# Building an edge-count matrix on TensorE: strips of 25 rows against pairs of strips of 12 rows

## The chip, the cores and the metric

One core of one Trainium2 chip runs the kernel. The metric is device time in microseconds (us). The kernel before takes 369.93 us, the median of 3 runs (369.87 to 371.19).

## The reference, cut to what matters

```python
# x [1250, 512]; src, dst [40000], dst sorted and denser at low rows (1250 * u**2)
h   = relu(layernorm(x) @ W1 + b1) @ W2 + b2          # 512 -> 256 -> 512
x   = x + h + segment_sum(h[dst], src, 1250)          # row = src, col = dst
n   = layernorm(x)
gate = softmax(n @ W_gate + b_gate); thr = sigmoid(n @ W_thr + b_thr) * 0.25
w   = max(gate - thr, 0); w = w / sum(w)
x   = x + sum_e w[:, e] * (n @ W_exp[e] + b_exp[e])   # 8 experts, 512 x 512
```

The segment sum is computed as a product with a count matrix A: A[d, s] is the number of edges from d to s, plus one on the diagonal for h itself. The kernel builds A from the edge list.

## The kernel before, in words

**Prologue** (L657 to L724 on VectorE, L1004 to L1046 on TensorE). The 40,000 edges lie in 320 chunks of 125. From each chunk's smallest and largest `dst` VectorE marks which chunks touch which block of 25 rows of A (`above`, `below`, `hit`, `hit_idx`), TensorE turns the marks, and a dozen tiny operations make a table `wtab`: for each block the first chunk and the number of steps. The keys of all edges (`src % 250` and `5 * dst + src // 250`) are turned to lie with an edge per partition (`keys`).

**Counting** (`compare` on VectorE, `count` on TensorE, `block_out` on ScalarE, a loop on SyncE). A is made in 50 blocks of 25 rows by 1250 columns. In PSUM such a block is [125, 250]: partition 5 * row + s // 250, column s % 250. For each chunk of a block VectorE compares the keys with two running-number tables (L771): `places[..][0:128]` gives a one-hot of the partition and `places[..][128:384]` one of the column, 384 elements a chunk, `int16` in, `float16` out, up to 4 chunks in an instruction. TensorE multiplies the two one-hots (L1108: 128 columns of weights, 250 moving columns) into a PSUM bank. `STEPS` says how many instructions of how many chunks a step has; a register loop runs the steps of the table. Eight one-hot buffers (`hot`) let VectorE run ahead by two to four blocks. L1100 adds the diagonal. ScalarE copies the finished block to one of five buffers `counts` (L525) and writes the positions of the block five places ahead (`positions`, L493); SyncE moves it by one DMA (L368) into its 25 rows of a tile of A, `a_t` (3 buffers of [125, 1250]).

**In between** stand, on TensorE, ten slots of the hidden layer (`next_slot`: L1056, L1058, L1029) in the first seven blocks, and from block 10 on the product of a finished tile with the hidden rows (`aggregate`, L1070, float32, six matmuls a tile, spread over five blocks); on VectorE the norms' statistics (`first_norm`), four block sums (`block_sum`) and the column sums of A (`column_sum`, L796). An aggregate of tile i starts with block 5 * i + 10. The order on each engine is written out by hand; there is no scheduler.

**After the last block** its DMA lands, VectorE adds the last tile to the column sums, TensorE makes the degrees (L1133) and the last aggregates, and the second layer, norm, gate and experts follow (from 142 us to the end), which the change leaves as they are.

The loop on SyncE, which the prediction speaks of:

```python
for w in range(NW):                                  # 50 blocks
    i, q = w // WPT, w % WPT
    sp.wait_ge(win_out, w + 1)
    ...
    sp.dma_start(a_t[i % 3][q * WIN:(q + 1) * WIN, :].rearrange("p (h l) -> p h l", h=HI),
                 counts[q][0:WIN * HI, :]).then_inc(win_moved[q], 16)
```

Of the kernel before, what the change touches and what calls it, by code (L numbers as in the profile page):

```python
# [30 lines left out]
def gnn_moe(nc, x, src, dst, W1, b1, W2, b2, Wg, bg, Wt, bt, We, be, out):  # L31
# [12 lines left out]
    WIN = 25  # L44
    HI = 5
    LO = 250
    SW = HI * LO
    WPT = 5
    NW = TILES * WPT
    PART = 4  # L50
    STEPS = ((1, (4, 4, 4, 4)), (2, (3, 3, 3, 3)), (4, (4, 4, 4, 4)), (6, (4, 4, 4)), (9, (4, 3, 3)), (18, (4, 4)),
             (30, (3, 3)), (NW, (3, 2)))
    FIXED = ((1, 2), (2, 1), (NW, 0))
    EARLY = 9
    LAG = 5
    AHEAD = FIXED[0][1] * sum(STEPS[0][1])
    PADS = AHEAD + sum(STEPS[0][1]) - 1
    SEG = 128
    SEGS = 3
    REC = 2 * SEGS  # L60
    HOT = SEGS * SEG
# [4 lines left out]
    assert R * TILES == N and R == WPT * WIN and SW == N and CH * EP == NE  # L66
    assert WIN * HI <= SEG and LO <= 2 * SEG and LO % WIN == 0 and 2 * HI == TILES
    assert D == BANK and ROWS <= 128 and CH <= BANK and KC * SW <= 5 * BANK
    assert (CH + PADS + 1) * REC * WORD < 2 ** 24 and (CH + PADS + 1) * REC < WORD and KC * SW <= 5 * BANK

    with ExitStack() as ctx:
# [36 lines left out]
        self_pos = sb("self_pos", [128, SEG + HI - 1], F16)  # L108
        self_lo = sb("self_lo", [128, 2 * LO - WIN], F16)


        iota_pos = sb("iota_pos", [EP, PART, SEG], I16)
        iota_lo = sb("iota_lo", [EP, 2 * SEG], I16)
        win_base = sb("win_base", [EP, NW])
        places_all = sb("places", [128, WPT * PART * HOT], I16)
        places = [places_all[0:EP, q * PART * HOT:(q + 1) * PART * HOT].rearrange("p (c h) -> p c h", c=PART) for q in range(WPT)]
        base_row = sb("base_row", [ROWS, NW])
        last_row = sb("last_row", [ROWS, NW])
        step_col = sb("step_col", [NW, 1])
        step_inv = sb("step_inv", [NW, 1])  # L120
        first_end = sb("first_end", [NW, 1])
        step_half = sb("step_half", [NW, 1])
# [31 lines left out]
        below = sb("below", [ROWS, GJ, NW])  # L154
        above = sb("above", [ROWS, GJ, NW])
        hit = sb("hit", [ROWS, GJ, NW])
        hit_idx = sb("hit_idx", [ROWS, 2, GJ, NW])
        wmax = sb("wmax", [NW, 2])
        wtmp = sb("wtmp", [NW, 1])
        wfirst = sb("wfirst", [NW, 1])  # L160
        wcount = sb("wcount", [NW, 1])
        wsteps = sb("wsteps", [NW, 1])
        wcols = sb("wcols", [NW, 3])
        wfirsts = sb("wfirsts", [1, NW])
        wtab = sb("wtab", [1, 2 * NW], I32)
        keys = sb("keys", [EP, (CH + PADS) * REC], I16)
        HOTS = 8
        split = sb("split", [128, HOTS * PART * HOT], F16)
        hot = [split[0:EP, b * PART * HOT:(b + 1) * PART * HOT].rearrange("p (c h) -> p c h", c=PART) for b in range(HOTS)]

# [5 lines left out]
        xn = [sb(f"xn{i}", [R, D]) for i in range(2)]  # L176
# [5 lines left out]
        counts = [sb(f"counts{i}", [SEG, LO]) for i in range(WPT)]  # L182
        late = sb("late", [128, 4 * SW])
        a_t = [late[0:R, i * SW:(i + 1) * SW] for i in range(3)]
        a_sum = late[0:R, 3 * SW:4 * SW]
        assert KD * N <= 4 * SW
# [13 lines left out]

        s_hi = places_all[:, 0:PAIRS * 4 * 2 * 128].bitcast(F16).rearrange("p (j c k t) -> p j c k t", j=PAIRS, c=4, k=2)
# [11 lines left out]
        assert 2 * KD * N <= HOTS * PART * HOT  # L213
        xhi = split[:, 0:KD * N].rearrange("p (k n) -> p k n", k=KD)
        xlo = split[:, KD * N:2 * KD * N].rearrange("p (k n) -> p k n", k=KD)
        assert 2 * KD * N + 128 <= HOTS * PART * HOT
# [28 lines left out]
        lo_ready, self_base, self_ready = sem("lo_ready"), sem("self_base"), sem("self_ready")  # L245
# [3 lines left out]
        wcols_ready, wrows_ready, wtab_ready = sem("wcols_ready"), sem("wrows_ready"), sem("wtab_ready")  # L249
# [3 lines left out]
        first_ready = sem("first_ready")  # L253
        x_turned, x_t_ready = sem("x_turned"), sem("x_t_ready")
        r_done, r_ready = sem("r_done"), sem("r_ready")
        pos_ready = sem("pos_ready")
        hot_ready = [sem(f"hot_ready{p}") for p in range(4)]
        hot_used = [sem(f"hot_used{p}") for p in range(4)]
        step_base, step_ready, step_prep = sem("step_base"), sem("step_ready"), sem("step_prep")
        win_done, win_out = sem("win_done"), sem("win_out")  # L260
        win_moved = [sem(f"win_moved{q}") for q in range(WPT)]
# [24 lines left out]
        CONSTS = 7  # L286
# [12 lines left out]
        def parts_of(w):  # L299

            return next(parts for end, parts in STEPS if w < end)

        def fixed_of(w):

            return next(n for end, n in FIXED if w < end)

        def hot_at(w, p):

            if w < EARLY:
                return 4 * (w % 2) + p  # L310
            return 2 * ((w - EARLY + 2) % 4) + p

        def freed_by(w):

            return w - 2 if w < EARLY + 2 else w - 3 if w < EARLY + 4 else w - 4

        def moved(eng, tile):

            for q in range(WPT):
                eng.wait_ge(win_moved[q], 16 * (tile + 1))  # L320
# [17 lines left out]
        def _(sp):  # L338
# [973 lines left out]
```

## Time and profile before

| | |
|---|---|
| median of 3 runs | 369.93 us (369.87 to 371.19) |
| the profiled execution, its own time | 369.96 us |
| its span on the core | 368.2 us |
| busy share of the span: TensorE, VectorE, ScalarE, GpSimd | 95%, 85%, 35%, 15% |
| first compare / last `counts` copy / last strip landed | 13.7 / 131.6 / 137.9 us |

Times in the trace count from the start of the span. A busy share is an average over stages. TensorE's busy time counts overlapping matmuls as pipelined, so the distance between starts says more than a record's length. SPq, DVEq and PEq are the sequencers of SyncE, VectorE and TensorE: what they spend on registers, table loads and on issuing DMAs.

### The profile page before, as it was taken

What the parts mean: (1) busy time and instruction counts of PE and PEld (TensorE: products, weight loads), DVE (VectorE), ACT (ScalarE), POOL (GpSimd) and SP (SyncE); (2) the same over time, 40 slices, a digit from 0 to 9 for tenths busy, and PEclk for the clock granted to TensorE, in tenths of its full rate; (3) what the DMA queues carried; (4) which work ended last, traced back from release to release, by engine and by line L of the source; (5) the groups of instructions that cost most, each with busy time, mean ns of one, the idle gap of its engine ahead of it and who ended that gap; (6) DMA issues with size and microseconds to landing.
All of it is one profiled execution on the core that took longest, in us unless ns stands there. A gap on an engine that the chain in (4) does not pass through costs nothing.

```text
span 368.2 us, 7339 instructions
## 1 busy us (share of the span) xinstructions
PE 351.1 (95%) x2542; PEld 269.7 (73%) x2542; DVE 314.0 (85%) x565; ACT 127.9 (35%) x224; POOL 56.2 (15%) x83
## 2 busy tenths in 40 slices
PE   2999999999999989999999999999999999999995
PEld 1777787656656645457767888888888888888884
DVE  6799997999999878898686888889888888888764
ACT  5844354655679502377731313003030030210000
POOL 7000000000000000063632313050140500500000
PEclk9999999999999999999999999999999999999999
DMA  8971010222222250003000003030030300000133
GB/s 223 214 239 39 16 42 29 74 68 76 79 74 78 84 170 6 0 2 121 3 0 2 0 6 112 0 116 2 1 116 2 114 2 1 2 2 0 44 119 121
DMA packets 16273, 22.06 MB, mean 60 GB/s; under 512 B 2188, under 2 KB 9235, under 8 KB 16236
## 3 DMA queue, kind: packets, MB, share of 16 engines
q1 hardware_dynamic: 15820, 21.05, 19.4%
q10 hardware_dynamic: 416, 0.53, 0.6%
q8 instruction: 21, 0.34, 0.4%
q14 instruction: 16, 0.13, 0.1%
HBM read 12.77 MB, written 2.56 MB: 42 GB/s over the span
## 4 chain that ended last, share of the span: by engine, by line
PE 81%; DVE 10%; issue 3%; DMA 2%; DVEq 2%; ACT 1%; ACTq 0%
PE ps_g L1220 10%; PE ps_g L1221 10%; PE ps_g L1222 10%; PE ps_w L1108 9%; PE ps_g L1070 9%; DVE split L771 3%; PE ps_g L1056 3%; PE ps_a L1220 2%; PE ps_a L1222 2%; PE ps_a L1221 2%; PE ps_w L1221 2%; PE ps_w L1222 2%; PE ps_w L1220 2%; PE ps_g L1146 2%; DVE x_sb L854 2%
## 5 line engine op out<-in xcount | busy, mean ns | idle before, releaser
L771 DVE TENSOR_TENSOR split<-places,keys 125x1536 f16<-125x1536 int16 (+2 forms) x125 | 91.0, 794 | 4.3 <-PE ps_w L1108 1.9
L944 DVE SCALAR_TENSOR_TENSOR x_sb<-ps_g,weight_s,x_sb 125x256 f32<-125x256 f32 (+1 forms) x142 | 75.1, 546 | 19.6 <-PE ps_g L1222 18.4
L1220 PE MATMUL ps_g<-wb_hi,places 128*128 128x256 f16 x212 | 57.8, 273 | 0.1
L1221 PE MATMUL ps_g<-wb_lo,places 128*128 128x256 f16 x212 | 57.8, 273 | 0.0
L1222 PE MATMUL ps_g<-wb_hi,r_sb 128*128 128x256 f16 x212 | 57.8, 273 | 0.0
L1108 PE MATMUL ps_w<-split 125*128 125x250 f16 x402 | 53.7, 270 | 2.4 <-DVE split L771 1.8
L1108 PEld LDWEIGHTS ps_w<-split 125*128 125x128 f16 x402 | 36.7, 97 | 21.0 <-DVE split L771 8.4
L1070 PE MATMUL ps_g<-late,r_sb 125*128 125x512 f32 (+3 forms) x120 | 49.3, 516 | 1.7 <-DMA late<-counts 1.7
L574 ACT ACTIVATE wb_hi<-stage 128x512 f16<-128x512 f32 x7 | 4.4, 628 | 99.1 <-PE ps_g L1222 48.8
L1220 PE MATMUL ps_g<-wb_hi,split 128*128 128x256 f16 x142 | 38.7, 273 | 0.0
L1222 PE MATMUL ps_g<-wb_hi,split 128*128 128x256 f16 x142 | 38.7, 273 | 0.0
L1221 PE MATMUL ps_g<-wb_lo,split 128*128 128x256 f16 x142 | 38.7, 273 | 0.0
L493 ACT ACTIVATE places<-iota_pos,win_base 125x512 int16<-125x512 int16 x50 | 35.7, 714 | 0.0
L525 ACT ACTIVATE counts<-ps_w 128x250 f32<-128x250 f32 x50 | 19.0, 379 | 28.5 <-PE ps_g L1070 23.5
L1070 PEld LDWEIGHTS ps_g<-late,r_sb 125*128 125x128 f32 x120 | 19.5, 191 | 9.7 <-issue 9.0
L1220 PEld LDWEIGHTS ps_g<-wb_hi,places 128*128 128x128 f16 x212 | 20.8, 98 | 3.2 <-DVE x_sb L944 0.6
L442 POOL TENSOR_TENSOR t_sum<-stage 128x512 f32<-128x512 f32 x6 | 7.6, 1273 | 99.5 <-DVE wb_lo L837 87.1
L1221 PEld LDWEIGHTS ps_g<-wb_lo,places 128*128 128x128 f16 x212 | 20.7, 98 | 2.6
L1222 PEld LDWEIGHTS ps_g<-wb_hi,r_sb 128*128 128x128 f16 x212 | 20.7, 98 | 2.4
L944 DVE SCALAR_TENSOR_TENSOR x_sb<-ps_a,weight_s,x_sb 125x256 f32<-125x256 f32 x36 | 17.3, 481 | 4.3 <-PE ps_a L1222 3.7
L1056 PE MATMUL ps_g<-w_sb,x_t 128*125 128x256 f32 x80 | 19.6, 388 | 0.0
L465 POOL MEMSET split<- 128x4 f16 x1 | 0.1, 102 | 124.1 <-ACT counts L525 124.1
(223 smaller groups left out, 665.5 us busy)
## 6 DMA issues: line engine op xcount, KB each, us to landing
stage<-in_L_ffn_W_exp_dram SPq DMA_DIRECT2D x8, 1024.0 KB, 6.0
late<-counts SPq DMA_DIRECT2D x50, 122.1 KB
x_sb<-in_x_dram SPq DMA_DIRECT2D x5, 448.0 KB, 10.3
out_dram<-x_sb SPq DMA_DIRECT2D x10, 224.0 KB
w_sb<-in_L_gnn_W_dram SPq DMA_DIRECT2D x2, 512.0 KB, 10.0
out_dram<-x_sb ACTq DMA_DIRECT2D x10, 26.0 KB
b_sb<-in_L_gnn_b_dram SPq DMA_DIRECT2D x1, 250.0 KB
x_sb<-in_x_dram ACTq DMA_DIRECT2D x1, 208.0 KB
```

Of the source, the lines that this page charges most:

```text
L442: nc.gpsimd.tensor_tensor(t_sum[:, T1 - T1, :, :], b12, b11, ALU.subtract).then_inc(t_added, 1)
L493: nc.scalar.activation(places[w % WPT][:, :, 0:SEG], iota_pos[:, :, :], ACT.Identity, bias=win_base[:, w:w + 1], scale=1.0).then_inc(pos_r ...
L525: nc.scalar.activation(counts[q][:, :], ps_w[w % 2][:, 0:LO], ACT.Copy).then_inc(win_out, 1)
L771: nc.vector.tensor_tensor(hot[hot_at(w, p)][:, 0:n, :].rearrange("p c (k x j) -> p (c k) x j", k=SEGS, j=2), places[w % WPT][:, 0:n, :].re ...
L854: nc.vector.scalar_tensor_tensor(out=x_sb[:, i, :], in0=b2_sb[:, :], scalar=deg1[:, i:i + 1], in1=x_sb[:, i, :], op0=ALU.mult, op1=ALU.add ...
L944: nc.vector.scalar_tensor_tensor(out=x_sb[:, i, a:z], in0=bank[0:R, at:at + z - a], scalar=weight_s[:, expert_of(u), i:i + 1], in1=x_sb[:, ...
L1056: nc.tensor.matmul(r_bank[i % 2], x_t[i % XTS][:, k, :], w1_sb[:, k, :], start=(k == 0), stop=False)
L1070: g = nc.tensor.matmul(ps_g[:, a:z], r_sb[:, i, c * 128:(c + 1) * 128], a_t[i % 3][:, a - c * SW:z - c * SW], start=opens, stop=False, ski ...
L1108: mm = nc.tensor.matmul(bank[:, 0:LO], hot[hot_at(w, p)][:, c, 0:SEG], hot[hot_at(w, p)][:, c, SEG:SEG + LO], start=False, stop=False, ski ...
L1220: nc.tensor.matmul(out_cols, hi_x, wb_hi[par][:, q, k, :], start=(opens and k == 0), stop=False, skip_group_check=True)
L1221: nc.tensor.matmul(out_cols, hi_x, wb_lo[par][:, q, k, :], start=False, stop=False, skip_group_check=True)
L1222: mm = nc.tensor.matmul(out_cols, lo_x, wb_hi[par][:, q, k, :], start=False, stop=(k == 1), skip_group_check=True)
```

## The change

A is cut the other way. The source index is split in ten parts of 125 (`LO`, `HI`), so a strip of 12 rows by 1250 columns is a PSUM area of [120, 125], and two strips lie side by side in one bank: 54 groups, 50 of them with 24 rows, the first two and the last with one strip. A chunk needs 2 * 126 compared elements a strip, and its matmul has 125 moving columns. Both strips of a pair walk through the chunks with one loop: strip b starts a fixed number of chunks behind strip a (`behind`), and the table holds their common beginning.

A running number per partition is enough for both halves of the one-hot: `places_of` reads the same table twice, at 0 and at 10 * row. So the 50 `positions` writes and five `low_places` go, and ScalarE instead extends a table of 12,606 numbers in pieces of 700, five ahead of time and thirteen between blocks. A strip can straddle two tiles of 125 rows; it is then moved by two DMAs.

```diff
-    WIN = 25
-    HI = 5
-    LO = 250
+    WIN = 12
+    HI = 10
+    LO = 125
...
+    FIXED = ((1, 2, (6, 6)), (2, 1, (4, 4)))
+    LOOP = ((1, (5, 5), 0), (2, (4, 4), 0), (3, (6,), 11), (4, (5,), 9), (5, (4,), 7), (10, (6,), 5), (13, (5,), 4),
+            (30, (4,), 3), (NG - 1, (3,), 2), (NG, (2,), 0))
...
+        def windows_of(g):
+
+            return (2 * g,) if g in (0, 1, NG - 1) else (2 * g, 2 * g + 1)
...
-            for w in range(NW):
-                i, q = w // WPT, w % WPT
-                sp.wait_ge(win_out, w + 1)
-                if q == 0 and i >= 3:
-                    sp.wait_ge(g_done, i - 2)
-                    sp.wait_ge(a_summed, max(i - 3, 1))
-                sp.dma_start(a_t[i % 3][q * WIN:(q + 1) * WIN, :].rearrange("p (h l) -> p h l", h=HI),
-                             counts[q][0:WIN * HI, :]).then_inc(win_moved[q], 16)
+            for g in range(NG):
+                q = g % RINGS
+                sp.wait_ge(win_out, g + 1)
+                for s, a, z, tile, at in MOVES[g]:
+                    if tile > begun:
+                        begun = tile
+                        sp.wait_ge(g_done, tile - 2)
+                        sp.wait_ge(a_summed, max(tile - 3, 1))
+                    sp.dma_start(a_t[tile % 3][at:at + z - a, :].rearrange("p (h l) -> p h l", h=HI),
+                                 counts[q][SHIFT + a * HI:SHIFT + z * HI, s * LO:(s + 1) * LO]).then_inc(win_moved[q], 16)
...
+            def table(k):
+                a, z = k * PIECE, min((k + 1) * PIECE, TABLE)
+                nc.scalar.activation(places_all[:, a:z], places_all[:, 0:z - a], ACT.Identity, bias=piece_base[:, k:k + 1],
+                                     scale=1.0).then_inc(places_ready, 1)
...
+            def places_of(v, n):
+
+                base = places_all[0:EP, 0:SEG]
+                return bass.AP(base.tensor, base.offset, [list(base.ap[0]), [0, n], [row_of(v) * HI, SEGS], [2, SEG // 2], [1, 2]])
...
+                        nc.vector.tensor_tensor(hot[hot_at(stage, p)][:, 0:n, :].rearrange("p c (k x j) -> p c k x j", k=SEGS, j=2),
+                                                places_of(windows[s], n),
+                                                keys[:, ds(key_at, n * REC)].rearrange("p (c k j) -> p c k j", k=SEGS, j=2).unsqueeze(3)
+                                                .broadcast_to([EP, n, SEGS, SEG // 2, 2]),
+                                                ALU.is_equal).then_inc(hot_ready[p], 1)
...
+                            mm = nc.tensor.matmul(bank[:, s * LO:(s + 1) * LO], one_hots[:, c, HOT - 128:HOT], one_hots[:, c, 0:LO],
+                                                  start=False, stop=False, skip_group_check=True)
```

The prologue changes with it. The marks are made for 108 strips (elements 200 to 432 in each of five operations). The chain of tiny operations on columns that ended in three small matmuls is now one reduction, two small matmuls, and ten operations on one partition (216, 108 or 54 elements), all behind the matmuls. The constants of the table are written by 31 small memsets on VectorE, at its very start, and 30 on GpSimd.

SyncE's program, around the DMAs of the counts. Before, one a block:

```order
L358 DMA bg_sb<-in_L_ffn_b_thr_dram 125x1
L349 DMA stage<-in_L_ffn_W_exp_dram 128x4x512 x2
L368 DMA late<-counts 25x5x250 x50
L349 DMA stage<-in_L_ffn_W_exp_dram 128x4x512
L375 DMA early<-in_L_ffn_b_exp_dram 8x512 x3
L349 DMA stage<-in_L_ffn_W_exp_dram 128x4x512 x5
```

and now:

```order
L409 DMA bg_sb<-in_L_ffn_b_thr_dram 125x1
L400 DMA stage<-in_L_ffn_W_exp_dram 128x4x512 x2
L422 DMA late<-counts 12x10x125 x10
L422 DMA late<-counts 5x10x125
L422 DMA late<-counts 7x10x125
L422 DMA late<-counts 12x10x125 x9
L422 DMA late<-counts 10x10x125
L422 DMA late<-counts 2x10x125
```

The pattern goes on to the end of the strips: 114 DMAs in place of 50.

TensorE's program in a late block, with a piece of the aggregate. Before:

```order
L1070 MATMUL ps_g<-late,r_sb 128x226
L1100 MATMUL ps_w<-self_lo,self_pos 128x250
L1116 TENSOR_LOAD wtab
L1116 UNCONDITIONAL_BRANCH
L1108 MATMUL ps_w<-split 128x250 x5
L1111 ISA
L1116 COMPARE_AND_BRANCH
L1070 MATMUL ps_g<-late,r_sb 128x286
```

and now, where a group straddles two tiles (L1153 is there only then):

```order
L1117 MATMUL ps_g<-late,r_sb 128x452
L1149 MATMUL ps_w<-self_lo,self_pos 128x250
L1153 MATMUL ps_w<-self_lo,self_pos 128x250
L1179 TENSOR_LOAD wtab
L1179 UNCONDITIONAL_BRANCH
L1168 MATMUL ps_w<-split 128x125 x6
L1171 ISA
L1179 COMPARE_AND_BRANCH
L1117 MATMUL ps_g<-late,r_sb 128x512
```

Five matmuls of 250 columns for 25 rows have become six of 125 for 24 rows; the rest of a block is the same.

## Rows read from the trace of the kernel before

**Rows 1.** The page, busy time of each engine over the span.

```profile
PE 351.1 (95%) x2542; PEld 269.7 (73%) x2542; DVE 314.0 (85%) x565; ACT 127.9 (35%) x224; POOL 56.2 (15%) x83
```

**Rows 2.** Windows: length; busy us of PE, PEld, DVE, ACT, POOL; clock, DMA share, GB/s.

```profile
12.60:42.00 29.40, 27.81 (x177) 21.85 (x176) 27.59 (x48) 14.52 (x31) 0.00 (x0) 1.00 0.46 132
42.00:61.80 19.80, 19.53 (x124) 15.86 (x122) 18.46 (x26) 9.26 (x24) 0.00 (x0) 1.00 0.13 36
61.80:100.00 38.20, 37.97 (x238) 24.44 (x236) 37.61 (x48) 22.29 (x46) 0.00 (x0) 1.00 0.24 70
100.00:132.00 32.00, 30.90 (x170) 19.01 (x169) 29.99 (x45) 22.34 (x42) 0.00 (x1) 1.00 0.27 81
```

**Rows 3.** Chain that ended last, in order of time: start us, us, what.

```profile
0.74 2.48 DMA dst_i<-in_dst_dram
...
122.33 0.54 PE ps_w L1108 x5
122.86 1.62 PE ps_g L1070 x4
...
131.97 5.90 DMA late<-counts
```

**Rows 4.** Groups by form, VectorE, 12 to 140 us: busy, mean ns.

```profile
L771 DVE TENSOR_TENSOR split<-places,keys 125x1536 f16<-125x1536 int16 x47 | 41.8, 951 | 3.4 <-PE ps_w L1108 1.9 <-ACT places L488 1.1 <-issue 0.3
L771 DVE TENSOR_TENSOR split<-places,keys 125x1152 f16<-125x1152 int16 x58 | 41.0, 751 | 0.9 <-issue 0.7
L796 DVE TENSOR_TENSOR late<-late 125x1250 f32<-125x1250 f32 x9 | 13.1, 1456 | 3.5 <-DMA late<-counts 3.5
L771 DVE TENSOR_TENSOR split<-places,keys 125x768 f16<-125x768 int16 x20 | 11.0, 550 | 0.0
```

**Rows 5.** Lines L368 and L383, SyncE's issues: ns min/median/max, first and last start.

```profile
L368 SPq DMA_DIRECT2D late<-counts x50: 742/742/931, 32.9 to 132.0; - x50
...
L383 SPq DMA_DIRECT2D out_dram<-x_sb x10: 317/317/359, 347.3 to 364.9; - x10
```

**Rows 6.** Timeline of VectorE, prologue and first compares: start us, us, what.

```profile
4.61 0.36 DVE L665 TENSOR_TENSOR above<-last_row,cmin 80x200 f32<-80x200 f32 x1
...
10.34 0.20 DVE L698 SCALAR_TENSOR_TENSOR wcount<-wmax,wfirst,ones 50x1 f32<-50x1 f32 x1
10.58 0.21 DVE L702 SCALAR_TENSOR_TENSOR wsteps<-wcount,step_half,step_inv 50x1 f32<-50x1 f32 x1
...
12.40 0.19 DVE L713 SCALAR_TENSOR_TENSOR wtab<-ps_a,wfirsts 1x50 int32<-1x50 f32 x1
13.68 3.56 DVE L771 TENSOR_TENSOR split<-places,keys 125x1536 f16<-125x1536 int16 x4 [1.09 <-ACT places L488]
17.16 1.21 DVE L744 SCALAR_TENSOR_TENSOR w_sb<-ps_g,w_sb 128x1024 f32<-128x1024 f32 x1
```

**Rows 7.** Timeline of TensorE, the gate's matmuls of 18 and 9 columns.

```profile
157.62 0.35 PE L1165 MATMUL ps_g<-wg,split 128*125 128x18 f16 x4
157.82 0.38 PE L1168 MATMUL ps_g<-wg,split 128*125 128x9 f16 x4
```

**Rows 8.** Lines L1108 and L1165, their weight loads: ns min/median/max.

```profile
L1108 PEld LDWEIGHTS ps_w<-split x402: 95/98/101, 15.1 to 130.2; 125*128 125x128 f16 x134
...
L1165 PEld LDWEIGHTS ps_g<-wg,split x40: 136/138/139, 157.2 to 182.9; 128*125 128x125 f16 x40
```

**Rows 9.** Timeline of SyncE's queue at the start.

```profile
0.74 0.38 SPq L339 DMA_DIRECT2D dst_i<-in_dst_dram  x1
1.18 0.41 SPq L340 DMA_DIRECT2D src_i<-in_src_dram  x1
```

**Rows 10.** Timeline of TensorE, the matmul that closes block 6.

```profile
59.18 0.17 PE L1123 MATMUL ps_w<-zeros 1*128 1x2 f16 x1
```

**Rows 11.** Windows of one us, columns as in rows 2, counting and tail.

```profile
125.00:126.00 1.00, 1.00 (x6) 0.41 (x5) 1.00 (x3) 0.00 (x0) 0.00 (x0) 1.00 0.33 106
...
136.00:137.00 1.00, 0.42 (x2) 0.00 (x0) 0.00 (x0) 0.00 (x0) 0.00 (x0) 1.00 1.05 374
```

More of the change, by code:

```diff
@@ L185, in gnn_moe @@
         a_sum = late[0:R, 3 * SW:4 * SW]
+        below, above, hit = (late[0:ROWS, k * GJ * NV:(k + 1) * GJ * NV].rearrange("p (j v) -> p j v", j=GJ) for k in range(3))
+        hit_idx = late[0:ROWS, 3 * GJ * NV:5 * GJ * NV].rearrange("p (a j v) -> p a j v", a=2, j=GJ)
         assert KD * N <= 4 * SW
@@ new lines, in row_of, with fixed_of, loop_of, size_of @@
+        def row_of(v):
+            return WIN * (v // 2) if v < 4 else WIN * (v - 2)
+        def fixed_of(g):
+            return next(((n, tuple((0, m) for m in parts)) for end, n, parts in FIXED if g < end), (0, ()))
+        def loop_of(g):
+            parts = next(parts for end, parts, behind in LOOP if g < end)
+            return tuple((s, m) for s in range(len(windows_of(g))) for m in parts)
+        def size_of(parts):
+            return sum(m for s, m in parts if s == 0)
+        def stage_of(g):
+            return g + sum(n for end, n, parts in FIXED if end <= g)
@@ new lines, in hot_at, with group_rows @@
+        def hot_at(stage, p):
+            return 2 * (stage % 4) + p
+        def group_rows(fill, *rows):
+            a = 0
+            for end, parts, behind in LOOP:
+                n, ahead = sum(parts), fixed_of(a)[0] * size_of(fixed_of(a)[1])
+                value_of = {"add_a": (n - 1) / 2.0 - CH - ahead, "add_b": (n - 1) / 2.0 - CH - ahead - behind, "first_b": float(behind),
+                            "inv": 1.0 / n, "size": float(n * REC * WORD), "base": float((FRONT + CH + ahead) * REC * (WORD + 1))}
+                for row, name in rows:
+                    fill(row, value_of[name], a, end)
+                a = end
@@ new lines, in behind_of, with table_part @@
+        def behind_of(g):
+            return next(behind for end, parts, behind in LOOP if g < end)
+        def table_part(g):
+            return -(-(row_of(windows_of(g)[-1]) * HI + SEG) // PIECE)
+        MOVES, MOVED, MOVED_BY, LAST = [], [], {}, {}
+        total = [0] * RINGS
+        for g in range(NG):
+            moves = []
+            for s, v in enumerate(windows_of(g)):
+                row, end = row_of(v), min(row_of(v) + WIN, N)
+                while row < end:
+                    z = min(end, (row // R + 1) * R)
+                    moves.append((s, row - row_of(v), z - row_of(v), row // R, row % R))
+                    row = z
+            MOVES.append(moves)
+            total[g % RINGS] += 16 * len(moves)
+            MOVED.append(total[g % RINGS])
+            for s, a, z, tile, at in moves:
+                LAST[tile] = g
+                MOVED_BY[tile] = list(total)
@@ L317, in moved @@
         def moved(eng, tile):
-            for q in range(WPT):
-                eng.wait_ge(win_moved[q], 16 * (tile + 1))
+            for q in range(RINGS):
+                eng.wait_ge(win_moved[q], MOVED_BY[tile][q])
         PRODUCT, READ = {}, {}
@@ L414, in _ @@
[L414 to L424 removed]
+            nc.gpsimd.memset(keys[:, 0:FRONT * REC], -1).then_inc(pads_ready, 1)
@@ L1120, in _ @@
-            for w in range(NW):
-                count(w)
-                if w < WPT + LAG:
-                    nc.tensor.matmul(ps_w[w % 2][:, 0:2], zeros[0:1, 0:128], zeros[0:1, 0:2], start=False, stop=True,
+                stage = stage_of(g)
+                steps, parts = fixed_of(g)
+                for f in range(steps):
+                    one_step(stage, parts)
+                    stage = stage + 1
+                    next_slot()
+                with pe.Fori(0, pe.value_load(wtab[0:1, NG + g:NG + g + 1])):
+                    one_step(stage, loop_of(g))
@@ new lines, in _ @@
+            pe.wait_ge(self_ready, 4)
+            begins = [LAST[i] + LAG for i in range(TILES)]
+            pieces = {}
+            for i in range(TILES - 1):
+                for n in range(len(cuts)):
+                    pieces.setdefault(begins[i] + min(n, 4), []).append((i, n))
+            for g in range(NG):
+                count(g)
+                if g not in pieces:
+                    nc.tensor.matmul(ps_w[g % 2][:, 0:2], zeros[0:1, 0:128], zeros[0:1, 0:2], start=False, stop=True,
```

434 lines of the change are left out of this document (208 added, 226 removed).

## The prediction, made before the changed kernel ran

> **What bounds the kernel now.** I read the page's busy times first: TensorE 95%, VectorE 85%, ScalarE and GpSimd far behind [rows 1]. That is an average, so the windows come next. The change touches 0 to 138 us, and there they show two engines that are both nearly full in each stretch: 27.8 and 27.6 us of 29.4, then 38.0 and 37.6 of 38.2, and 30.9 and 30.0 of the last 32.0 [rows 2]. The granted clock is 1.00, the level of 2.4 GHz, throughout. The chain of waits tells which of the two is last: up to about 42 us compares and norms on VectorE, from then on TensorE, where a late block is 0.54 us of counting and a piece of the aggregate, and at the end the last DMA, 5.90 us [rows 3]. The groups by form give VectorE's share: 125 compares, and an idle time before them of only 4.3 us in all [rows 4]. So a gain needs both engines relieved, and this change relieves both. Then I looked at who comes next. SyncE issues one DMA a block, each holds its queue for 0.742 us, 37.1 us in 99.8 [rows 5]. Nothing waits for it today.
>
> **Part 1, the prologue: later by 3.6 us.** Each of the five mark operations grows from 200 to 432 elements. 200 elements of float32 take 0.36 us and 1024 take 1.21, so an element costs 1.03 ns and each operation 0.24 us more [rows 6]: 1.2 us, all ahead of the keys, on which TensorE's transposes and then the small matmuls wait. Behind these matmuls stood 0.43 us of work (12.16 to 12.59); now there are eight operations that depend on each other. A dependent pair starts 0.24 us apart [rows 6]; with 0.22, 0.11 and six times 0.06 us for the elements, and two side operations of 0.13, that makes 2.9 us, 2.4 more. The seven tiny operations that go from ahead of the matmuls free nothing, as TensorE was turning x until then. The 31 memsets stand where VectorE waits for `dst` (0.74 to 3.22 us): 0.08 us each fits, 0.12 would cost 1.3 us. I take 0 and keep 1.3 for the range. GpSimd's 30 memsets and ScalarE's first five pieces are needed at 12 us or later, where both idled. The first compare moves from 13.7 to 17.3.
>
> **Part 2, compares: VectorE 18.4 us less.** The inputs are fixed, so the strips' chunks can be counted: 125 compares and 402 matmuls before, as the rows have, and 119 and 476 now. Records of 951, 751 and 550 ns for 4, 3 and 2 chunks [rows 4] give 0.20 us for 384 elements, 0.52 ns each, and 0.15 of fixed time, of which the next one covers 0.08: four records in a row take 3.48 us, 0.87 each [rows 6]. Before: 47 * 0.87 + 58 * 0.67 + 20 * 0.47 = 89.2 us. Now a chunk is 252 elements, 0.131 us: 18 of six chunks at 0.86, 12 of five at 0.73, 42 of four at 0.60, 46 of three at 0.46 and one of two: 70.8 us. This takes the rate for granted though the pattern has one dimension more; see rival D.
>
> **Part 3, counting on TensorE: 14.5 us less.** Five matmuls of 250 columns take 0.54 us [rows 3], 0.107 each, so 402 are 43.0 us. No row has 125 columns with new weights each time. From above the bound is 0.107. From below: 18 columns with loads of 138 ns start 0.05 us apart [rows 7, 8], and half of 250 columns is 0.052. Here loads are the shorter kind, 98 ns [rows 8]. I take 0.057, by the streaming time plus a little: 27.1 us, 15.9 less. Four more groups and nine straddling ones add 13 diagonals of 0.107. The Trainium skill (TensorE: Matmul & The Clock Gate, Back-to-back issue gap) gives about 81 ns for load and matmul pairs of 128 columns; by it counting would be 38.6 us, and only 3 us would be gained here. The gate's rows are against it, though they are eight in a row at most.
>
> **Part 4, ScalarE: nothing.** 50 position writes and five tables go, 18 pieces come. It was busy 35% [rows 1]; no wait of VectorE on positions stands in the chain after the start.
>
> **Part 5, SyncE: 50 DMAs become 114.** This is the step that I think decides. A pair of strips is two DMAs, and a strip that straddles two tiles three for its group. Price: the row of the same transfer, 0.742 us [rows 5], plus 0.04 between issues, as 1.18 stands to 0.74 + 0.38 [rows 9]: 0.785. The pattern (rows of the tile from ten partitions each) is the same kind, 12 rows from 120 partitions for 25 from 125. The nearest rows on either side are 0.317 (an output, both sides plain) and 0.931 (the first of the counts) [rows 5]. I take 0.742, since it was the median and the minimum of 50 of the same sort. From group 6 on that is 104 DMAs, 81.6 us. When is group 6 out? Block 6 closed at 59.2 [rows 10], with VectorE setting the pace. Its compares for these rows fall from 30.2 (27 of four chunks, 10 of three) to 19.4 us, and the start is 3.6 later: 52.0. So SyncE ends its issues at 133.6, the last one starts at 132.8. VectorE and TensorE would have been done at 117: 131.6 + 3.6 - 18.4 for the one, and much the same for the other. They wait: TensorE for PSUM banks, ScalarE for one of five buffers, these for SyncE.
>
> The Trainium skill (DMA: Bandwidth & Descriptors, Issuing engines are not separate DMA queues) calls the time to initiate a DMA "usually small relative to the DMA itself". By that it would not bind, which is rival B. The row says 0.742 us each, and a tile of 125 rows needs 11.4 of them, 8.9 us, where TensorE needs about 6.7 (31 * 0.057 + 0.6 + 4.2 of aggregates).
>
> **Part 6, the tail: 3.3 us less from a faster landing.** Today the last DMA takes 5.90 us, and in the stretch before it the engines' share is 0.33 while it can be 1.05 [rows 11]. A third is 5 of 16 engines, full all the time. The Trainium skill (DMA: Bandwidth & Descriptors, Why a DMA increments its semaphore by 16 and not by 1) says that a DMA runs on the largest number up to 16 that divides both outer sizes: 5 for 25 and 125, agreeing with the share, and 12 for 12 and 120. Bounds: 5.90 us, and 2.48 for a plain load on an idle queue [rows 3]. I take 2.5, for the last one has 20 packets and nothing queued: landed at 135.3 in place of 137.9.
>
> **The sum.** The landing of the last strip releases the last column sum, the degrees and all that follows, and nothing behind it changes. 135.3 - 137.9 = -2.6 us on the profiled execution's own 369.96 (which is within 0.03 of the median): **367.4 us**.
>
> **The rivals.**
>
> A, the forecast, chance 0.44: SyncE's issues set the pace at about today's price. 362 to 372 us, by 0.70 to 0.78 us an issue.
>
> B, chance 0.26: the issue is cheaper, as more engines with fewer packets each are served. Below 0.62 us a DMA SyncE keeps up, and the engines' savings come through: 3.6 - 18.4 with the landing's 2.6 gives **353 us**. For it: the price differs by the kind of transfer, 0.317 to 0.742 [rows 5]. Against: nothing shows what of the transfer makes it 0.742.
>
> C, the other side, chance 0.18: the issue is dearer, as it grows with the number of engines served (12 for 5). From 0.81 us a DMA (issue and gap) the landing is at 137.9 or later and the gain is gone; at the bound of 0.931 the 104 DMAs take 101 us, 19.4 more, **387 us**.
>
> D, chance 0.05: the compare's pattern of four dimensions falls to half the rate. 476 * 252 elements at 0.52 ns more are 62 us, on VectorE all visible: 353 + 62 = **415 us**. Against: pairs of 16-bit neighbours are kept on all three sides, as before.
>
> E, chance 0.07: counting does not get cheaper on TensorE, and a matmul of 125 columns takes 0.107 like one of 250. The change then doesn't do what it says: 476 * 0.107 is 50.9 us, 7.9 more than before, and with the prologue the end moves by about 9 less 2.6: **376 us**. By the 81 ns of the Trainium skill (TensorE: Matmul & The Clock Gate) it would be 11.5 us above B's TensorE, 364, or hidden in A.
>
> **How the numbers follow.** Half a per cent, 1.85 us, is about what a measurement of this kernel can tell from no change. A lies around 367.4 on both sides of that bound: 0.26 below 368.1, 0.12 within, 0.06 above. With B all faster, a hundredth each of C and E below the line, and the rest of C, D and E slower: faster 0.54, same 0.12, slower 0.34. The range reaches from B, 353 with a microsecond to spare, to 380: half of C (0.09), D and a little of E lie above, some 0.03 below. A's own range is 362 to 372.
>
> **What would show it.** Right: SyncE's row for the counts shows 114 issues of about 0.74 us one behind the other from about 52 us on; TensorE and VectorE show gaps of 20% or more in 60 to 130 us, ending with ScalarE's copies that wait for landed strips; compares of 1512 elements take 0.94 us, of 756 0.54; the first compare starts at 17.3; counting matmuls start 0.057 us apart; the last DMA takes 2.5 us. Wrong: issues well under 0.6 us and the last copy near 117 (B), or above 0.8 (C); records of 1.6 us for 1512 elements (D); starts of 0.1 us between counting matmuls (E). If the first compare is later than 18.6 us, the prologue was priced too low.

## The result, and the profile after

The changed kernel takes 383.04 us (median of 4 runs, 382.25 to 383.48) where the kernel before takes 370.06 us beside it: a ratio of 1.0342, with a 95% interval of 1.0314 to 1.0369. It is slower by 13.0 us. The prediction was 367.4 us, with a range of 352 to 380, and faster as the likeliest sign. Number and sign are wrong. The profiled execution took 383.21 us, with a span of 381.4 us.

The page has less work and more time. Busy times of the changed kernel, against [rows 1]:

```profile
PE 348.6 (91%) x2629; PEld 266.3 (70%) x2629; DVE 299.9 (79%) x588; ACT 106.6 (28%) x193; POOL 54.7 (14%) x102
...
PEclk9999999999998995799999999999999999999999
```

VectorE lost 14.1 us of work and TensorE 2.5, although part of TensorE's was done at half the clock: the second row is its granted clock in 40 slices (9 is 90% or more of 2.4 GHz), and the slices from 143 to 162 us have 5 and 7 where the kernel before has 9 throughout. The windows say where the engines stood still; the columns are those of [rows 2]:

```profile
12.60:42.00 29.40, 25.83 (x185) 21.91 (x185) 23.11 (x51) 9.83 (x26) 0.00 (x0) 1.00 0.48 136
42.00:61.80 19.80, 17.43 (x153) 14.13 (x151) 16.35 (x23) 7.41 (x19) 0.00 (x0) 1.00 0.13 32
61.80:100.00 38.20, 34.10 (x267) 20.77 (x264) 32.50 (x52) 16.70 (x35) 0.00 (x0) 1.00 0.27 66
100.00:132.00 32.00, 27.47 (x169) 15.60 (x170) 22.47 (x40) 11.71 (x23) 0.00 (x0) 0.95 0.28 70
...
144.00:146.00 2.00, 0.20 (x1) 0.23 (x2) 0.26 (x1) 0.00 (x0) 0.00 (x0) 0.60 0.44 50
146.00:158.00 12.00, 12.00 (x32) 7.84 (x32) 6.84 (x12) 0.00 (x0) 0.00 (x0) 0.50 0.23 85
```

From 61.8 to 132 us TensorE idles 8.6 us of 70.2, where it idled 1.3 before, and VectorE 15.2. Neither is full any more. SyncE is, though the busy times don't count it. (The 0.95 is a first, short drop of the clock: 0.57 from 120 to 124 us, behind 2 us with 0.57 us of work. SyncE's issues go on back to back through it.) Its own line, against [rows 5], and who waited for those transfers:

```profile
L422 SPq DMA_DIRECT2D late<-counts x114: 652/772/1393, 30.4 to 143.5; - x114
...
  DVE late L843: 18.1, 7
  ACT counts L558: 7.7, 8
  PEld ps_g L1117: 4.7, 1
  PE ps_g L1117: 4.0, 1
```

The chain of work that ended last shows the same at the end of the counting (start us, us, what). Behind the copy six issues hang on one another before the last DMA starts; it lands, and the tail of the first layer runs:

```profile
138.34 0.39 ACT counts L558
138.73 0.66 SPq L422
139.39 0.04 issue
139.44 0.77 SPq L422
...
143.51 1.94 DMA late<-counts
145.45 0.35 issue
145.80 3.75 PE ps_g L1117 x4
149.56 4.00 PE ps_a L1203 x20
153.55 4.89 PE ps_g L1117 x8
...
158.47 0.39 ACT early L628
```

So two things are lost. The last strip lands at 145.5 us instead of 137.9 (+7.6). And from there to the first copy of the finished product (`early`) it is 13.0 us, where it was 6.9 (137.9 to 144.8): +6.1, because all of it runs at a granted clock of 0.50, the level of 1.2 GHz. The four aggregates that take 3.75 us took 1.96 before. Together they make 13.7 us; the span grew by 13.2.

### The profile page after: what moved, and what is told of

The parts are those of the page before. It is cut to its first block, busy times and chain, and to the rows that moved or that the text cites. A ratio compares the mean times of both kernels' runs of the same rounds, so it can differ in the third digit from the quotient of the medians.

```text
span 381.4 us, 7568 instructions
## 1 busy us (share of the span) xinstructions
PE 348.6 (91%) x2629; PEld 266.3 (70%) x2629; DVE 299.9 (79%) x588; ACT 106.6 (28%) x193; POOL 54.7 (14%) x102
## 4 chain that ended last, share of the span: by engine, by line
PE 86%; issue 4%; DVE 4%; DMA 2%; SPq 1%; ACT 1%; DVEq 1%; ACTq 0%
PE ps_g L1117 13%; PE ps_g L1290 10%; PE ps_g L1291 10%; PE ps_g L1292 10%; PE ps_w L1168 7%; PE ps_g L1103 4%; PE ps_g L1216 3%; PE ps_a L1290 2%; PE ps_a L1291 2%; PE ps_a L1292 2%; PE ps_w L1291 2%; PE ps_w L1290 2%; PE ps_w L1292 2%; PE ps_w L1149 2%; PE ps_g L1256 1%
## 5 line engine op out<-in xcount | busy, mean ns | idle before, releaser
L809 DVE TENSOR_TENSOR split<-places,keys 125x756 f16<-125x756 int16 (+4 forms) x119 | 73.3, 680 | 11.1 <-PE ps_w L1168 7.8
L1117 PE MATMUL ps_g<-late,r_sb 125*128 125x512 f32 (+3 forms) x120 | 57.0, 582 | 13.2 <-issue 9.1
L1168 PEld LDWEIGHTS ps_w<-split 125*128 125x128 f16 x476 | 30.2, 99 | 19.7 <-DVE split L809 10.6
L1168 PE MATMUL ps_w<-split 125*128 125x125 f16 x476 | 37.4, 220 | 6.5 <-DVE split L809 5.8
L1117 PEld LDWEIGHTS ps_g<-late,r_sb 125*128 125x128 f32 x120 | 21.3, 208 | 22.4 <-issue 21.9
L558 ACT ACTIVATE counts<-ps_w 128x250 f32<-128x250 f32 (+1 forms) x54 | 20.1, 374 | 53.2 <-PE ps_g L1117 40.2
L843 DVE TENSOR_TENSOR late<-late 125x1250 f32<-125x1250 f32 x9 | 13.1, 1461 | 19.7 <-DMA late<-counts 18.1
L992 DVE SCALAR_TENSOR_TENSOR x_sb<-ps_a,weight_s,x_sb 125x256 f32<-125x256 f32 x36 | 17.3, 482 | 4.3 <-PE ps_a L1292 3.7
L1103 PE MATMUL ps_g<-w_sb,x_t 128*125 128x256 f32 x80 | 19.7, 390 | 0.0
```

The source lines that it names most:

```text
L558: nc.scalar.activation(counts[q][:, 0:cols], ps_w[g % 2][:, 0:cols], ACT.Copy).then_inc(win_out, 1)
L809: nc.vector.tensor_tensor(hot[hot_at(stage, p)][:, 0:n, :].rearrange("p c (k x j) -> p c k x j", k=SEGS, j=2), places_of(windows[s], n), k ...
L843: nc.vector.tensor_tensor(a_sum, a_t[0] if i == 1 else a_sum, a_t[i % 3], ALU.add).then_inc(a_summed, 1)
L992: nc.vector.scalar_tensor_tensor(out=x_sb[:, i, a:z], in0=bank[0:R, at:at + z - a], scalar=weight_s[:, expert_of(u), i:i + 1], in1=x_sb[:, ...
L1103: nc.tensor.matmul(r_bank[i % 2], x_t[i % XTS][:, k, :], w1_sb[:, k, :], start=(k == 0), stop=False)
L1117: g = nc.tensor.matmul(ps_g[:, a:z], r_sb[:, i, c * 128:(c + 1) * 128], a_t[i % 3][:, a - c * SW:z - c * SW], start=opens, stop=False, ski ...
```

## The experiments

Each ratio is against runs of the kernel before on the same chip, whose median was 369.4 to 370.1 us in every case; 383.0 us is the changed kernel of the result. Landings and copies are from the profiled execution of each.

**Who issues.** Three kernels leave the 114 DMAs as they are and hand the second strip of a pair to another queue. The core of the edit is a function `move(eng, g, strips)` that holds SyncE's loop body:

```diff
+            for g in range(NG):
+                sp.wait_ge(win_out, g + 1)
+                move(sp, g, (0,))
```

The first adds, behind ScalarE's copy of a group g that has two strips:

```diff
+                act.wait_ge(win_out, g + 1)
+                move(act, g, (1,))
```

> The changed kernel, but the second strip of each pair is moved by a DMA that ScalarE issues behind its own copy; SyncE keeps the first strips. Nothing else differs: the same 114 DMAs, the same bytes. Theory (SyncE's serial issues set the end of counting from 61.4 us on, 0.81 us for each DMA, and the gaps they leave on TensorE lower its clock in the tail): SyncE has about 61 issues left instead of 114, its row is no longer back to back, the last DMA lands at 131 to 136 us instead of 145.5, the granted clock stays near 1.00 behind it, and the time is 360 to 367 us. Rival one (the moving itself is what is slow: more packets over fewer engines): who issues doesn't matter, 380 to 384 us. Rival two (the compares and TensorE wait for each other through the one semaphore per stage, and SyncE only follows): also 380 to 384 us.

Measured: 378.74 us, 1.0254 [1.0225, 1.0282]. A miss: 4.3 us gained where 16 to 23 were expected. The waits between 60 and 160 us show why (engine, operand and line waited for: us in total, times, longest):

```profile
ACT counts L564 <- PE ps_g L1126: 29.1, 24, 2.6
DVE split L818 <- PE ps_w L1177: 15.4, 24, 2.9
PEld ps_w L1158 <- ACT counts L564: 15.3, 21, 2.4
...
PE ps_w L1158 <- ACT counts L564: 7.1, 8, 2.0
```

TensorE now waits for ScalarE's copies, its weight loads 15.3 us and its matmuls 7.1 us (the two waits overlap, so they don't add up): on ScalarE copy, 0.38 us, and issue, 0.78 us, stand one behind the other, and the counting has only two PSUM banks. The last copy was made at 143.0 us, no earlier than SyncE alone had got to the end. What was gained is the clock (0.991 on average instead of 0.976): landing to `early` was short again, 7.0 us.

The second makes the copy of group g first and then issues the strip of the group before:

```diff
-                act.wait_ge(win_out, g + 1)
-                move(act, g, (1,))
+                act.wait_ge(win_out, g)
+                move(act, g - 1, (1,))
```

> As in the run with ScalarE issuing the second strips (378.7 us), but it first makes the copy of the next pair and only then issues the DMA of the last one, so that a copy never waits for its own strips' issue. Theory (that run was held back by the chain copy, issue, copy on ScalarE): TensorE's waits for copies fall by half or more, and the time is 363 to 372 us. Rival (ScalarE's 0.4 + 0.8 us for each pair hold TensorE's two banks however they are ordered): 376 to 380 us.

Measured: 369.64 us, 0.9994 [0.996, 1.0027]. The same DMAs, the same two queues, only the order of copy and issue turned, and 9.1 us less. The weight loads' wait for copies fell from 15.3 us to 10.1, the matmuls' own from 7.1 to 3.1. The last issue was at 135.1 us.

In the third it is `pool.wait_ge(win_out, g + 1)` and `move(pool, g, (1,))`, with semaphores of its own for GpSimd's transfers.

> The changed kernel, but GpSimd, which is idle in this stage, issues the DMA of each pair's second strip, with semaphores of its own; ScalarE only copies, SyncE issues 61 of the 114. Same DMAs, same bytes. Theory, mended after the run in which ScalarE issued them (there TensorE's waits moved from SyncE to ScalarE's chain of copy, 0.38 us, and issue, 0.78 us, one behind the other): with neither SyncE nor ScalarE in the way TensorE is the bound; it has 69.6 us of work left at 61.8, so the last strip lands at 132 to 136 us and the time is 361 to 367 us, if GpSimd's issue takes under 1.3 us. Rival (the moving is what is slow, whoever issues): 377 to 384 us. Rival (an issue of GpSimd costs 1.5 us or more): its row is back to back, and the time is above 375 us.

Measured: 366.30 us, 0.9906 [0.9873, 0.994]. GpSimd's issues cost less than SyncE's and neither row is back to back:

```profile
L386 SPq DMA_DIRECT2D late<-counts x59: 673/772/1060, 30.5 to 129.6; - x59
L386 POOL DMA_DIRECT2D late<-counts x55: 570/572/735, 43.9 to 128.8; - x55
```

The last issue was at 129.6 instead of 143.5 us, and TensorE was busy 37.3 of the 38.2 us from 61.8 to 100. With the same transfers and bytes, the rival that the moving itself is slow has fallen; 16.7 us hung on who issues.

**Fewer issues.** Two kernels drop DMAs of second strips and keep all computing, so that rows of the matrix are stale:

```diff
+            if g % 2 == 0 and g >= 18:
+                moves = [m for m in moves if m[0] == 0]
             MOVES.append(moves)
```

This leaves out 19; with `if g >= 18` alone it is 38.

> The changed kernel without the DMA of the second strip in every other pair from the 18th on: 19 of the 114 DMAs are left out, so that those rows of the count matrix are stale. Compares, matmuls and copies are all still made. Theory: each DMA left out takes its issue of 0.81 us off SyncE's chain, 15.4 us in all, as long as TensorE isn't the bound first; the last DMA lands at 130 to 136 us, and with the clock kept the time is 361 to 369 us. Rival (the handshake of VectorE and TensorE sets the pace): 380 to 384 us.

> The changed kernel without the second strip's DMAs from the 18th pair on: 38 of 114 are left out (19 in the run before of this kind, which took 365.6 us). Theory: SyncE is no longer near the bound, 38 issues of 0.81 us would be 31 us, but only some 11 to 14 us can be had, since TensorE is full then: 357 to 366 us, and little under the run with 19 left out. Rival (SyncE is the only bound down to there): 350 us or less.

Measured: 365.61 us, 0.9875 [0.9838, 0.9911], with 19 left out, and 365.96 us, 0.9884 [0.9828, 0.9939], with 38. The first 19 are worth 17.4 us, the next 19 nothing. In the profiled execution with 19 left out the last DMA lands at 134.1 instead of 145.5 us (11.4 of their 15.4 us of issue; the last copy, at 131.5, is now what it waits for), and landing to `early` takes 8.9 instead of 13.0 us. That is the floor at which TensorE binds (busy 36.3 of the 38.2 us from 61.8 to 100), and GpSimd's version stands on it.

**The same bound in the kernel before.** There each block's DMA is cut by rows:

```diff
-                sp.dma_start(a_t[i % 3][q * WIN:(q + 1) * WIN, :].rearrange("p (h l) -> p h l", h=HI),
-                             counts[q][0:WIN * HI, :]).then_inc(win_moved[q], 16)
+                for a, z in ((0, 8), (8, 16), (16, WIN)):
+                    sp.dma_start(a_t[i % 3][q * WIN + a:q * WIN + z, :].rearrange("p (h l) -> p h l", h=HI),
+                                 counts[q][a * HI:z * HI, :]).then_inc(win_moved[q], 16)
```

> The kernel before with each block's one DMA cut into three by rows (8, 8 and 9 rows of the matrix): 150 DMAs instead of 50, the same bytes, everything else the same. Theory (an issue costs SyncE about 0.74 us plus 0.04 whatever it moves, one after the other): 43 blocks are left at 59 us, 129 issues at 0.78 to 0.81 make 101 to 105 us, so the last DMA lands near 162 us instead of 138, and the time is 390 to 402 us. Rival (an issue's price goes with the partitions or bytes that it describes): at a third of 0.74 us the row is as before, and the time is 369 to 373 us.

Measured: 399.68 us, 1.0814 [1.0781, 1.0847].

```profile
L369 SPq DMA_DIRECT2D late<-counts x150: 668/693/832, 32.8 to 160.9; - x150
...
  ACT counts L526: 35.0, 27
  DVE late L797: 29.4, 7
```

A third of the partitions costs 0.693 us instead of 0.742. Between these two the price is one for each DMA and hardly goes with what it moves. 132 issues start between 59.8 and 160.9 us, 0.77 apart, and ScalarE and VectorE, who waited for almost nothing here before, now wait for landed strips.

> The kernel before with the DMAs of every second block issued by GpSimd. SyncE has 25 issues there instead of 50 and waited for nobody. Theory (more issuers help only where SyncE's issues are the bound): no change, 368 to 371 us. Rival (GpSimd's queue lands DMAs faster, or relieves something else, whatever the kernel): 362 to 366 us, which would take the gain of the run with GpSimd in the changed kernel away from the theory.

Measured: 373.80 us (370.51 to 375.76), 1.0122 [1.0082, 1.0161]. GpSimd as a second issuer brings no gain where SyncE wasn't the bound, so the gain in the changed kernel isn't some virtue of that queue. That it costs 1.2% was not expected. The four times go with their mean granted clocks (0.999 at 370.5 us, 0.984 at 375.8); why it falls more often here is open. The groups show the compares as long as before, 951 ns for 1536 elements.

**The start of SyncE's stretch.** In the changed kernel the hidden layer's matmuls are cut to a quarter of their depth:

```diff
-                for k in range(KD):
+                for k in range(1):
                     nc.tensor.matmul(r_bank[i % 2], x_t[i % XTS][:, k, :], w1_sb[:, k, :], start=(k == 0), stop=False)
```

> The changed kernel with the hidden layer's matmuls cut to the first of their four parts of the depth, so that its values are wrong and each of the ten slots between the early groups costs TensorE about 1.2 us less (8 float32 records of 1.99 us become 2 of 0.5). Theory: in the changed kernel TensorE's slots, one behind each early group and 3.3 us long, set when the group of 60.2 us is out, and SyncE's back-to-back stretch starts there; so that copy comes 6 to 9 us earlier, the last DMA lands as much earlier (137 to 140 instead of 145.5), and the time is 374 to 378 us. Rival (VectorE's compares or the keys set the first stage, as the prediction took it): the copy stays within 2 us of 60, and the time at 381 to 384 us. Rival (SyncE doesn't set the second stage): the copy moves, the landing doesn't.

Measured: 379.07 us, 1.0267 [1.0228, 1.0305]; against the changed kernel 4 us less, short of the 5 to 9 expected. The copy of group 7 came at 54.19 instead of 60.18 us, as expected, but the last issue at 140.5, only 3.0 earlier. Groups 8 and 9, which have no slot ahead of them, still came 2.3 and 2.6 us apart, because VectorE's compares and block sums now set the pace (TensorE, and its wait for the compares in brackets):

```profile
54.03 0.28 PE L1149 MATMUL ps_w<-self_lo,self_pos 128*128 128x250 f16 x1
54.95 0.50 PE L1168 MATMUL ps_w<-split 125*128 125x125 f16 x6 [0.64 <-DVE split L809]
55.80 0.50 PE L1168 MATMUL ps_w<-split 125*128 125x125 f16 x6 [0.35 <-DVE split L809]
```

SyncE could follow these; back to back it went from 59.6 us on, with 97 issues left instead of 101. That is 1.0 us of start and 3.3 of issues; 1.3 went again because the issues took a little more each (0.843 us apart instead of 0.829). So in the changed kernel TensorE's slots set when group 7 is out, and VectorE stands close behind them.

**The clock.** 33 matmuls on constants, read by nobody, fill two of TensorE's waits in the changed kernel, 10 ahead of tile 8's first aggregate and 23 ahead of tile 9's:

```diff
+                        for m in range(10):
+                            nc.tensor.matmul(ps_w[(g + 1) % 2][:, 0:384], self_pos[:, 0:128], self_lo[:, 0:384], start=True, stop=True)
...
+            for n in range(23):
+                nc.tensor.matmul(ps_w[0][:, 0:384], self_pos[:, 0:128], self_lo[:, 0:384], start=True, stop=True)
             aggregate(TILES - 1, 0, 2)
```

> The changed kernel with 33 matmuls of 384 columns on constants added, whose results nobody reads: 10 ahead of tile 8's first aggregate and 23 ahead of tile 9's, where TensorE stood waiting for DMAs. The DMAs are left as they are. Theory: the last DMA lands at 145 to 147 us as in the changed kernel, but the granted clock stays at 1.00 behind it, the first four aggregates of tile 9 take 2.0 us instead of 3.75, and the time falls by 5 to 6 us, to 377 or 378. Rival (the lower clock has another cause than the idle time, or costs nothing on the path): 382 to 384 us, clock at 0.50 as before.

Measured: 379.06 us, 1.0254 [1.0227, 1.0281]: 4.0 us less by work that is thrown away. The timeline of TensorE there:

```profile
142.35 3.90 PE L1206 MATMUL ps_w<-self_lo,self_pos 128*128 128x384 f16 x23
146.09 1.88 PE L1117 MATMUL ps_g<-late,r_sb 125*128 125x512 f32 x4
147.81 2.24 PE L1210 MATMUL ps_a<-ones,late 125*125 125x1 f32 x20
149.91 4.42 PE L1117 MATMUL ps_g<-late,r_sb 125*128 125x226 f32 x8
```

The last issue is at 143.4 as before; the four aggregates take 1.88 us, not 3.75, the degrees 2.24, not 4.20. `early` starts at 154.4 instead of 158.5. The time is 1 us above what was expected, for the clock did not stay up: the last eight ran mostly at the lower level, which is the part of 6.1 us that did not come back. And that fall has no gap ahead of it:

```profile
138.00:150.00 12.00, 12.00 (x63) 7.50 (x64) 9.33 (x12) 0.66 (x2) 0.26 (x4) 1.00 0.44 130
150.00:152.00 2.00, 2.00 (x7) 1.29 (x7) 1.88 (x4) 0.00 (x0) 0.00 (x0) 0.69 0.00 0
```

So the wait for the last strip explains 4.0 of the 6.1 us; the cause of the rest is open.

**What is left.** The version with GpSimd still fell to 0.50 between 138 and 144 us. Eight more such matmuls go into it, four ahead of tile 9's first aggregate and four behind its last.

> The run in which GpSimd issues the second strips (366.3 us), with 8 matmuls of 384 columns on constants whose results nobody reads: 4 ahead of tile 9's first aggregate, where TensorE waited 0.5 us, and 4 behind its last one, where it waits for the copies. There the clock had fallen to 0.50 from 138 to 144 us. Theory (the lower clock comes of too little work in TensorE's stretch before it): it stays at 1.00, the last aggregates and the second layer's first four matmuls are 3 us shorter together, less up to 1 us for what the eight matmuls delay: 363 to 365 us. Rival (another 0.7 us of work doesn't change the level): 366 to 367.5 us.

Measured: 364.95 us, 0.9878 [0.9847, 0.9909], clock 1.00 in the profiled execution, `early` at 139.2 instead of 140.4 us. In time it can't be told from the version without the eight (0.9906 [0.9873, 0.994]). The same kernel once more, beside the next one:

> The same kernel as the one with GpSimd's issues and 8 added matmuls (364.95 us, 0.9878 of the kernel before), once more, on the chip of the run beside it: 364 to 367 us, 0.984 to 0.992.

Measured: 365.79 us, 0.9907 [0.9869, 0.9945]. In this profiled execution the clock fell to 0.50 from 138 to 140 us in spite of the eight, and `early` came at 140.6: that they keep the clock up is not shown. Its windows before 62 us are those of the changed kernel: TensorE idles 5.8 us there, 5.7 of them in matmuls that wait for compares (the 12.3 us expected for the next run adds to these the weight loads' waits, which overlap them). The suspects are the groups with two steps, so their first step goes ahead of the loop:

```diff
-    FIXED = ((1, 2, (6, 6)), (2, 1, (4, 4)))
+    FIXED = ((1, 2, (6, 6)), (2, 1, (4, 4)), (3, 1, (6,)), (4, 1, (5,)), (5, 1, (4,)))
```

with `fixed_of` giving the parts of both strips, and slots and norms at fixed steps in groups 0 and 1 only.

> The version with GpSimd's issues and the 8 added matmuls (364.95 us), and in groups 2 to 4 the first of the two steps is taken out of the loop and gets a stage of buffers of its own, so that VectorE can write the second step while TensorE still has the first or the hidden layer's slot before it. Nothing is computed anew. Theory (in these three groups the two engines wait for each other, some 1.1 to 1.5 us of TensorE's idle time in each, 12.3 us on compares before 62 us in all): TensorE's waits for compares before 62 us fall by 3 to 4 us and the time to 361 to 363 us. Rival (VectorE is then late with the next groups, and the wait only moves): 364 to 366 us.

Measured: **360.54 us** (359.56 to 362.63), 0.9751 [0.9713, 0.9789], and 5.2 us under its neighbour. The waits before 62 us, first the neighbour's, then its own:

```profile
PEld ps_w L1179 <- DVE split L820: 7.2, 8, 1.8
DVE split L820 <- PE ps_w L1179: 7.2, 4, 2.7
...
PE ps_w L1179 <- DVE split L820: 5.7, 8, 1.4
```

```profile
PEld ps_w L1180 <- DVE split L820: 2.5, 3, 1.7
...
PE ps_w L1180 <- DVE split L820: 1.7, 2, 1.3
```

The copy of group 7, behind the last slot, comes at 55.3 instead of 60.2 us, and TensorE is busy 19.7 of 19.8 us from 42 to 61.8. This version beats both kernels, by 9.4 and about 22 us.

## Why the prediction was wrong

Its mechanism was the right one, rival A's and C's alike: SyncE's issues, one behind the other, set the end of the counting. It is shown from three sides (another issuer, fewer issues, the same bound made in the kernel before). Three steps of the sum failed: the start of SyncE's stretch in part 5 (with "VectorE setting the pace"), the price of an issue there, and "nothing behind it changes" in the sum. The first two alone turn the sign (378.0, with the landing 377.4 us); the third takes the time out of the range.

- **Part 5, the start, +6.2 us.** The text has group 6 out at 52.0 because VectorE's compares fall from 30.2 to 19.4 us, "with VectorE setting the pace". It didn't after the change, and the prediction's own reading of the chain had TensorE last from about 42 us on, so already in the kernel before block 6 stood on TensorE. The windows of the first stage had both engines nearly full [rows 2], and TensorE's ten slots of the hidden layer there, 2.3 to 2.7 us each, are not what the change removes. Group 6 was copied at 56.9 and group 7 at 60.2, where SyncE's stretch began, with 101 issues to go; the prediction's count has it there at 54.4. The run with shorter slots moved group 7 by 6.0 us, to 54.2, close to the 54.4 that the prediction had with VectorE's pace. And part of it is new: in groups 2 to 4 the steps of a loop share one stage of buffers, so each engine waits for the other. The last version got 4.9 us of that stage back by unrolling them.
- **Part 5, the price, +4.4 us.** 0.785 was assumed, 0.742 and a gap of 0.04. (The row that the gap was read from has 0.06: 1.18 less 0.74 and 0.38 [rows 9]. With it the price would have been 0.80.) The issue is 0.772 in the median, 0.03 above the row of before, and 0.04 lies between two, 0.812; with some issues of up to 1.39 us the 100 intervals from 60.58 to 143.51 average 0.829. The last issue starts at 143.5, not 132.8, and 10.7 is what these two terms make. Rival C put the point of no gain at 0.81 a DMA and its cause with the number of engines served; the cut blocks speak for a price nearly fixed for each DMA.
- **Part 6, the landing, -0.6 us.** 1.94 us against 2.5 predicted and 5.90 before. The gain is there, but the last DMA moves 2 rows of the matrix where it moved 25, so that more engines share a transfer is not what it shows.
- **The tail, +6.1 us, a term that the sum doesn't have.** "Nothing behind it changes" holds for the instructions, not for the clock. The prediction itself forecast gaps of 20% on TensorE and read a granted clock of 1.00 in every window [rows 2], but never asked what the gaps would do to it. TensorE had 0.20 us of work in 144 to 146 us and none in 142 to 144, and the clock then stood at 0.50 for 12 us. The run with fillers gave 4.0 us back; the rest went with a second fall, of which the cause is open. The Trainium skill (TensorE: Matmul & The Clock Gate, Part 1: The HAM clock gate) describes a gate that goes by how busy the engine has been recently. This trace agrees at the wait from 142 to 145.8 us; the fall of the run with fillers, behind 12 full us, is not explained by it.
- 367.4 + 6.2 + 4.4 - 0.6 + 6.1 is 383.5; the profiled execution took 383.2.
- **Part 1** was 0.7 us too high: the first compare came at 16.58 us, not 17.3. The 31 memsets cost nothing.
- **Part 2** held. The compares keep VectorE busy for 73.3 us against 91.0 before, 17.7 less where 18.4 were predicted, and rival D is out:

```profile
L809 DVE TENSOR_TENSOR split<-places,keys 125x1008 f16<-125x1008 int16 x42 | 25.6, 679 | 2.8 <-PE ps_w L1168 2.4 <-issue 0.2
L809 DVE TENSOR_TENSOR split<-places,keys 125x756 f16<-125x756 int16 x46 | 22.4, 549 | 1.7 <-issue 1.0 <-PE ps_w L1168 0.6
L809 DVE TENSOR_TENSOR split<-places,keys 125x1512 f16<-125x1512 int16 x18 | 16.2, 942 | 3.8 <-PE ps_w L1168 2.0 <-issue 1.7
```

- **Part 3** held: six counting matmuls of 125 columns take 0.33 us in the chain, 0.055 each against 0.057 predicted. Rival E is out. The 81 ns for a pair of load and matmul (the Trainium skill, TensorE: Matmul & The Clock Gate, Back-to-back issue gap) don't hold for these rows of six to twelve pairs; the measurement decides.
- **Part 4** held, ScalarE is at 28%.
- The rule set against part 5 (the Trainium skill, DMA: Bandwidth & Descriptors, Issuing engines are not separate DMA queues), that initiating is usually small beside the transfer, doesn't describe this case: 0.77 us of issue for transfers that land in 1.94 us (the last) or 2.61 (the one issued at 61.4 us).
- **Rival B's** 353 us was not to be had by cheaper issues. With issues out of the way the kernel takes 366 (three kernels, 365.6 to 366.3), and the last copy comes at 129.3 us (with GpSimd), not near 117. B's sum let all that VectorE saves come off the end. TensorE's slots and the handshake of groups 2 to 4 were not in it, and behind them TensorE hardly gained: late in the counting it takes 7.4 and 7.9 us from one tile's four-matmul piece to the next (102.13, 109.56, 117.49 with GpSimd's issues) where the kernel before takes 7.7 (107.45, 115.13) and the prediction counts 6.7. Counting a group fell from 0.54 to 0.33 us, but a tile has 5.2 groups for 5 blocks and more diagonals, and a two-matmul piece of the aggregate holds TensorE 0.92 us where it held it 0.86.

## What to carry to other kernels

An engine that only issues DMAs has a budget like any other: count its issues, multiply by the row's price with the gap, and set the product against the stretch in which they must go out. When a change splits transfers, look first for an idle engine that can issue some of them, and never put an issue ahead of a copy that somebody waits for. Where a new bound will leave TensorE idle, work out the time behind the wait at the lower clock too. And a saving on one engine moves a stage's end only if the other one's work in that stage was read as well.

## What the runs showed of the hardware

- The issue of a transfer between two SBUF places costs SyncE 0.69 us for 40 source partitions, 0.77 for 120 and 0.74 for 125 with rows of twice the bytes; ScalarE 0.78. GpSimd needs 0.57 us for the 120 (0.77 in the kernel before with 125), and the transfer lands 2.7 us (median) after. I had not expected GpSimd to be the cheapest.
- TensorE's granted clock fell to 0.50 behind a wait with next to no work (142 to 145.8 us of the changed kernel), and with 33 matmuls on constants in the waits it stayed at 1.00 behind the last one, until 150.8 us: 4.0 us of 383 for work that nobody reads. Not every gap did that: in the kernel before it stayed at 1.00 through 136 to 138 us, with 0.42 us of work, and with ScalarE's issues through 126 to 128, with 0.15.
- It also fell, for 6 us from 137.8 on, in the version with GpSimd's issues, though TensorE was busy for 1.6 us or more in every 2 us window from 124 us up to there. With eight matmuls more it stayed at 1.00 in one profiled execution and fell from 138 on in the other. In the last version it fell at 131.1 us, though TensorE was busy 1.74 us or more in every 2 us from 122 up to there. These falls, and the one at 150.8 us of the run with fillers, come during or within 1.3 us behind the 20 matmuls of one column that make the degrees; the kernel before has the same 20 and kept 1.00. What brings the clock down there is open.
